# Two of 88 gathered edge groups fetched row by row from the sync and scalar engines in a graph network kernel

## What is computed

```python
h = jnp.maximum(_layernorm(x, axis=-1), 0.0)
x = x + _L0_gnn_ref(h, edge_index, ...)          # three SAGE layers: mean of neighbours, two products each
h = jnp.maximum(_layernorm(x, axis=-1), 0.0)
# the GINE block, the "edge stage" of the kernel:
messages   = gelu((h[src] + edge_attr) @ We1 + be1) @ We2 + be2
aggregated = segment_sum(messages, dst)
x = x + gelu(((1 + eps) * h + aggregated) @ Wu1 + bu1) @ Wu2 + bu2
```

## Time and profile before

| | |
|---|---|
| time, median of 3 runs (lowest to highest) | 881.31 us (880.73 to 883.44) |
| time of the profiled execution | 883.02 us |
| its span, first to last instruction | 880.7 us |
| granted TensorE clock, mean over the span | 0.983 |
| TensorE busy | 827.7 us (94%) |
| VectorE busy | 694.9 us (79%) |
| ScalarE busy | 323.9 us (37%) |
| GpSimd busy | 385.3 us (44%) |

### The profile page before, as it was taken

How to read it: one execution, slowest core, us unless ns; L and a number is a source line. 1 busy time by engine, 2 the same in 40 slices (tenths; PEclk the granted TensorE clock), 3 DMA queues, 4 the chain that set the end, 5 groups by cost and what they waited for, 6 DMA issues and landing times.

```text
span 880.7 us, 14779 instructions
## 1 busy us (share of the span) xinstructions
PE 827.7 (94%) x4876; PEld 631.4 (72%) x4876; DVE 694.9 (79%) x1887; ACT 323.9 (37%) x570; POOL 385.3 (44%) x443
## 2 busy tenths in 40 slices
PE   3688999999999999999889999999999999999994
PEld 1243555555687787777667888888888888898883
DVE  8999999998255445455799989988979898987961
ACT  3566677776155555454111111111121111112111
POOL 1000000000022222232578777777777777777772
PEclk9979999999999999999889999999999999999998
DMA  4301010001000000010563344444443444434421
GB/s 112 120 2 13 3 15 14 14 3 25 1 1 1 1 1 12 13 59 18 130 194 115 114 138 120 123 131 146 138 138 111 138 138 122 139 112 138 138 75 41
DMA packets 37492, 67.50 MB, mean 77 GB/s; under 512 B 14729, under 2 KB 24932, under 8 KB 37156
## 3 DMA queue, kind: packets, MB, share of 16 engines
q1 hardware_dynamic: 26276, 43.68, 16.6%
q0 software_dynamic: 11136, 22.83, 9.7%
HBM read 63.18 MB, written 3.30 MB: 75 GB/s over the span
## 4 chain that ended last, share of the span: by engine, by line
PE 41%; POOL 29%; DVE 13%; issue 11%; DMA 4%; ACT 1%; SPq 0%; POOLq 0%; ACTq 0%; DVEq 0%
POOL f_adj L653 29%; PE f_ps L1328 16%; PE f_ps L1321 10%; PE f_ps L1226 3%; PE f_ps L1219 2%; PE f_ps L1383 2%; DVE f_select L945 2%; PE f_ps L1295 2%; DVE f_region L722 2%; DMA inv<-f_rstd 2%; DVE f_region L720 2%; PE f_ps L1257 1%; DVE f_region L726 1%; DVE f_region L724 1%; PE f_ps L1425 1%
## 5 line engine op out<-in xcount | busy, mean ns | idle before, releaser
L653 POOL DMA_INDIRECT f_adj<-table,f_by_edge x348 | 333.4, 958 | 106.9 <-issue 103.9
L945 DVE TENSOR_SCALAR f_select<-f_ps 128x512 fp32r<-128x512 f32 x425 | 260.5, 678 | 6.6 <-PE f_ps L1383 6.0
L1383 PE MATMUL f_ps<-f_select,f_pair 125*128 125x512 f32 x850 | 220.8, 407 | 5.3 <-DVE f_select L945 5.2
L638 POOL CAST f_wide<-f_adj 125x500 fp32r<-125x500 uint8 (+1 forms) x70 | 40.6, 580 | 358.1 <-ACT f_adj L1091 212.4
L1383 PEld LDWEIGHTS f_ps<-f_select,f_pair 125*128 125x128 f32 x850 | 155.7, 190 | 44.7 <-issue 8.5
L1205 ACT ACTIVATE f_adj<-f_adj 128x512 f32<-128x512 f32 (+1 forms) x88 | 55.1, 626 | 306.4 <-DVE f_adj L1061 256.6
L1328 PE MATMUL f_ps<-f_wide,f_pair 125*128 125x500 f32 (+1 forms) x700 | 162.5, 385 | 1.5 <-DVE f_wide L777 0.6
L1091 ACT CAST f_adj<-f_ps 128x500 f32 x213 | 126.0, 592 | 55.8 <-PE f_ps L1226 43.4
L1328 PEld LDWEIGHTS f_ps<-f_wide,f_pair 125*128 125x128 f32 x700 | 122.2, 189 | 33.5 <-issue 6.2
L1425 PEld LDWEIGHTS f_ps<-f_adj 128*128 128x128 f32 x984 | 119.4, 192 | 13.1 <-issue 11.1
L1321 PE MATMUL f_ps<-f_adj,f_parts 125*128 125x500 fp8e4 (+1 forms) x525 | 128.5, 354 | 0.0
(11 more groups left out here) (149 smaller groups left out, 717.0 us busy)
## 6 DMA issues: line engine op xcount, KB each, us to landing
f_region<-in_edge_attr_T SPq DMA_DIRECT2D x33, 768.0 KB
f_adj<-table,f_by_edge POOLq DMA_INDIRECT x348
f_src_rows<-in_src_row SPq DMA_DIRECT2D x16, 256.0 KB, 4.7
f_xT<-in_xT SPq DMA_DIRECT2D x1, 1562.5 KB, 6.4
f_adj<-inv SPq DMA_DIRECT2D x1, 1562.5 KB, 9.4
out<-f_xT SPq DMA_DIRECT2D x6, 250.0 KB, 3.3
table<-f_region SPq DMA_DIRECT2D x6, 224.0 KB
f_rcntT<-inv SPq DMA_DIRECT2D x5, 250.0 KB, 3.7
```

What stands on the lines that cost most here:

```text
L653: pool.indirect_dma_start(out=rows[:, r % RW, j * D:(j + 1) * D], out_offset=None, in_=table, in_offset=bass.IndirectOffsetOnAxis(ap=table ...
L945: ins = dve.tensor_scalar(select[:, u % SELECT, :], offset, float(b * NP - CENTRE), None, ALU.is_equal)
L1383: ins = pe.matmul(z_columns(g), chosen[0:NP, p, b, :], select[0:NP, u % SELECT, :], start=b == 0 and p == 0, stop=b == NB - 1 and p == 1, ...
```

## The change

Groups 91 and 98 (`FAR`) no longer come by indirect DMAs, so GpSimd has 340 of them instead of 348. Each of their 1,024 rows comes by a DMA of its own, 1 partition x 128 floats, into a new buffer `far`.

```diff
+    FAR = [G - 14, G - 7]
+    FROM, UNTIL, BATCH = 2, G - 16, 8
+    ON_SP, FEW = 1, 4
...
+        far, o = carve(flat, o, (len(FAR), T * D), F32)
...
+            for i, g in enumerate(FAR):
+                sp.dma_start(far_idx[1:2, i * T * P:(i + 1) * T * P],
+                             t["src_row"][s.tile(g) * P:s.tile(g + 1) * P].rearrange("(a n) -> a n", a=1)
+                             ).then_inc(far_in, 16)
             sp.dma_start(inv.rearrange("(b p) -> p b", p=NP), rstd[0:NP, :],
...
+            def fetch_rows(k):
+                _, at_rows = nc.values_load_multi_w_load_instructions(
+                    far_idx[1:2, k * BATCH:(k + 1) * BATCH], engines=[mybir.EngineType.SP], min_val=0, max_val=N - 1,
...
+                for n, row in enumerate(at_rows, k * BATCH):
+                    i, j, p = n // (T * P), n // P % T, n % P
+                    sp.dma_start(far[p:p + 1, i, j * D:(j + 1) * D], table[bass.ds(row, 1), :]).then_inc(fetched[i], 16)
+
+            sp.wait_ge(far_in, 16 * len(FAR))
+            batches = ON_SP * T * P // BATCH
             for g in range(END):
+                if FROM <= g < UNTIL:
+                    for k in range((g - FROM) * batches // (UNTIL - FROM), (g - FROM + 1) * batches // (UNTIL - FROM)):
+                        fetch_rows(k)
...
-                if g in s.picked:
+                if g in s.picked or g in FAR:
                     continue
...
+                        if g in FAR:
+                            dve.wait_ge(fetched[FAR.index(g)], 16 * T * P)
+                            fetched_rows = far[:, FAR.index(g), 0:w]
...
+            few_from, few = ON_SP * T * P // FEW, (FAR_ROWS - ON_SP * T * P) // FEW
             for g in range(END):
+                if g == FROM:
+                    act.wait_ge(far_in, 16 * len(FAR))
+                if FROM <= g < UNTIL:
+                    for k in range((g - FROM) * few // (UNTIL - FROM), (g - FROM + 1) * few // (UNTIL - FROM)):
+                        fetch_rows(few_from + k)
                 for c in node_due(g, TAKE):
```

More of the change, by code:

```diff
@@ L251, in fast_path @@
     FLAG, KEEP = 12, 13
+    FAR = [G - 14, G - 7]
+    FROM, UNTIL, BATCH = 2, G - 16, 8
+    ON_SP, FEW = 1, 4
+    FAR_ROWS = sum(s.tiles(g) for g in FAR) * P
+    assert not any(g in s.picked or s.tiles(g) < T or g < UNTIL for g in FAR)
     with ExitStack() as ctx:
@@ L325, in fast_path @@
         viol, o = carve(flat, o, (4 * NT + 2 * G,), F32)
+        assert FAR_ROWS <= 4 * NT + 2 * G
+        far_idx = viol[:, 0:FAR_ROWS].bitcast(I32)
         bound, o = carve(flat, o, (2, G), F32)
@@ L378, in fast_path @@
             sem("node_added"), sem("stored"))
+        far_in, fetched = sem("far_in"), [sem(f"fetched{i}") for i in range(len(FAR))]
         tile_in, dst_tile_in, abs_ready = sem("tile_in"), sem("dst_tile_in"), sem("abs_ready")
@@ L587, in _ @@
             sp.dma_start(order[0:EP, 1, :], t["dst_next"]).then_inc(order_in, 16)
+            def fetch_rows(k):
+                _, at_rows = nc.values_load_multi_w_load_instructions(
+                    far_idx[1:2, k * BATCH:(k + 1) * BATCH], engines=[mybir.EngineType.SP], min_val=0, max_val=N - 1,
+                    skip_runtime_bounds_check_because="sources are node indices, as for the indirect DMAs")
+                for n, row in enumerate(at_rows, k * BATCH):
[3 more added lines that the diff above has]
+            batches = ON_SP * T * P // BATCH
             for g in range(END):
+                if FROM <= g < UNTIL:
+                    for k in range((g - FROM) * batches // (UNTIL - FROM), (g - FROM + 1) * batches // (UNTIL - FROM)):
+                        fetch_rows(k)
                 if g % PER == PER - 1 and EA < g // PER + EA < UNITS:
@@ L1057, in _ @@
                         dve.wait_ge(z_ready, g + 1)
-                        dve.wait_ge(gathered[r % RW], 16 * sum(s.tiles(s.of_ordinal(q)) for q in range(r % RW, r + 1, RW)))
+                        if g in FAR:
+                            dve.wait_ge(fetched[FAR.index(g)], 16 * T * P)
+                            fetched_rows = far[:, FAR.index(g), 0:w]
+                        else:
+                            gathers = [s.of_ordinal(q) for q in range(r % RW, r + 1, RW)]
+                            dve.wait_ge(gathered[r % RW], 16 * sum(s.tiles(h) for h in gathers if h not in FAR))
+                            fetched_rows = rows[:, r % RW, 0:w]
                         if r >= PR:
                             dve.wait_ge(msg_ready, s.of_ordinal(r - PR) + 1)
-                        dve.tensor_tensor(pre[:, r % PR, 0:w], z_group(g), rows[:, r % RW, 0:w],
+                        dve.tensor_tensor(pre[:, r % PR, 0:w], z_group(g), fetched_rows,
                                           ALU.add).then_inc(pre_ready, 1)
@@ L1181, in _, with fetch_rows @@
                     act.copy(part(chosen, 0, c), grow_rows(c)).then_inc(high3, 1)
-            for g in range(END):
+            def fetch_rows(k):
+                _, at_rows = nc.values_load_multi_w_load_instructions(
+                    far_idx[1:2, k * FEW:(k + 1) * FEW], engines=[mybir.EngineType.Activation], min_val=0, max_val=N - 1,
+                    skip_runtime_bounds_check_because="sources are node indices, as for the indirect DMAs")
+                for n, row in enumerate(at_rows, k * FEW):
+                    i, j, p = n // (T * P), n // P % T, n % P
+                    act.dma_start(far[p:p + 1, i, j * D:(j + 1) * D], table[bass.ds(row, 1), :]
+                                  ).then_inc(fetched[i], 16)
+            few_from, few = ON_SP * T * P // FEW, (FAR_ROWS - ON_SP * T * P) // FEW
+            for g in range(END):
+                if g == FROM:
[3 more added lines that the diff above has]
+                        fetch_rows(few_from + k)
                 for c in node_due(g, TAKE):
```

## The result

The changed kernel takes 915.72 us at the median (915.38 to 915.93, 4 runs) where the kernel before takes 882.13 (880.73 to 883.44, 4 runs) on the same chip: a ratio of 1.0377 [1.0363, 1.0392], 33.6 us slower. The forecast was 912 us, slower with 0.72.

The account below looks back on a forecast made before the run. TensorE was taken as the bound, only 3.0 us of its waits being winnable. The sum -3.0 + 33 + 0 = +30 on 883.0 us profiled gave 913 to 914, the median 1.7 lower: 912 us, range 878 to 948.

Parts of the forecast that it names:

- The bound of the gain, -3.0 us: At the end, eight gathers less save TensorE at most its 3.0 us of waits for the last messages.
- A batch on the scalar engine, 2.31 us: Scalar engine's sequencer: one register load (0.31 us) and four row issues (0.50 us each) take 2.31 us.
- The windows that are too short: From start of message h - 3 to picked group h's first product, batches don't fit at eleven of fifteen groups: 40 us.
- The place in the window: TensorE waits mostly at the first product behind the scalar engine's copy, which comes 2.8 us late at group 64.
- The size, +33 us: Late copies at eleven picked groups cost TensorE 40 us, less 7 us as the next windows open earlier.
- That the cost has a threshold: Scalar engine's batches: under 1.05 us each no window is too short; at 1.3 us copies are 3.0 us late.
- the issuing is hidden: Rival: batches fall into the scalar engine's 256.6 us of waits for the vector engine, leaving -3.0: 878 us; chance 0.14.
- SP at 0: SP's 64 batches, 276 us, are hidden in its 362.3 us wait for TensorE ahead of edge-attribute loads: 0 us.
- the queues at 0: DMA queues: 1,024 more packets, 91 us if one engine takes them all, are wanted only at groups 91 and 98: 0.
- The rule of the Trainium skill: By it the scalar engine's issuing would cost close to nothing, sum -3.0; the prediction went by the trace's rows instead.

Follow-up runs that it names:

- e3_no_fetch: Changed kernel with no row issued: two bulk loads of stand-in table rows fill `far` for groups 91 and 98; 879.82 us, 0.9977 of the kernel before.
- e1_sp_only: Changed kernel with group 98 given back to the gathers; only group 91's 512 rows are issued, by SP; 879.76 us, 0.9977 of the kernel before.
- e5_half_rows: Changed kernel with 64 scalar-engine batches instead of 128 over the same turns, stand-in rows for the rest; 880.59 us, 0.998 of the kernel before.
- e8_fixed_rows: Changed kernel with the scalar engine's 512 DMAs taking fixed table rows, without register load or address operation; 880.97 us, 0.998 of the kernel before.
- e9_split_640_384: e7_quiet_turns with 640 rows on SP and 384 on the scalar engine; 884.52 us, 1.0017 of the kernel before.
- e2_act_only: Changed kernel with group 91 given back to the gathers; only group 98's 512 rows are issued, by the scalar engine; 914.26 us, 1.0382 of the kernel before.
- e4_long_turns: Changed kernel with the scalar engine's 128 batches kept out of each picked group's turn and the turn ahead of it; 917.04 us, 1.0401 of the kernel before.
- e7_quiet_turns: Changed kernel with 768 rows on SP, 256 on the scalar engine, there only in turns where neither group nor next two are picked; 922.22 us, 1.0455.
- e6_sixteen_picked: e7_quiet_turns with 16 picked groups instead of 17; 923.23 us, 1.046 of the kernel before.
- e10_split_sixteen: e9_split_640_384 with 16 picked groups instead of 17; 884.37 us, 1.0015 of the kernel before.

## Why the prediction was right, and where it was not

- **The bound of the gain, -3.0 us: right.** Rows that cost nothing (`e3_no_fetch`) gain 2.1 us at the median, 3.1 in the span, though the last gather starts 10.7 us earlier. TensorE, not the engine that was relieved, is what the end depends on.
- **A batch on the scalar engine, 2.31 us: right, from parts that were not.** It takes 2.2 to 2.4. The address is 37 + 29 ns, not 147; an issue is 214 ns, not 290 (the first of a batch 446); but the register load grows with what it loads, 502 ns for four numbers where one took 278. The errors cancel, rounding too: the prediction's own terms add up to 0.52 us a row and 2.39 a batch, and it went on with 0.50 and 2.31. The Trainium skill (DMA: Bandwidth & Descriptors, Latency and other measured facts) has a floor of about 600 ns under a tensor_load; the loads of four rows here go down to 320 ns, those of eight are at 720.
- **The windows that are too short: right.** In both traces each window can be measured, from the start of message h - 3 to the first product. The eleven that the prediction found too short (9, 15, 27, 33, 45, 52, 58, 64, 76, 82, 88) grew by 5.6, 4.4, 5.2, 3.6, 2.1, 1.7, 1.9, 2.1, 5.3, 3.9 and 2.0 us, 38 in all where the sum said 40; of the other four only the one at 70 grew (0.9).
- **The place in the window, wrong.** "TensorE gets the copy 2.8 us late" and "most of it at the first product behind a copy" was the step that failed: 15.7 us are waited one step earlier, at the `flip`, for the gelu, and 4.9 at the product behind the copy. The batches of h - 2 and h - 1 already stand ahead of the gelu, and the prediction tested the window only at its end. That the waits at the `flip` are eleven as well is chance: they stand at nine of these groups and at 3 and 70, and none at 52 and 88.
- **The size, +33 us: the total right, its make-up not.** TensorE's idle time in the stage grows from 451 - 432.89 = 18.1 us to 484 - 444.80 = 39.2, so by 21 us, not by 33. The other 12 are matmuls that take longer. The 2,681 matmuls of the stage come in the same order in both traces, so they can be compared one by one: 7.3 us stand in those that overlap time at the lower clock (the sums above, 10.3 less 3.6, make this about 7 us), a term that the prediction didn't have, and 4.6 us in the 21 that follow a wait only after the change, 0.22 us each, since they no longer overlap with the one ahead of them. Without the clock's 7 us the loss would be some 27 us, an estimate from these figures; that the total comes within 4 us of the forecast is in part luck. That the lapses come from the waits is argued from where they stand, right behind late gelus and copies, and was not tried by itself. The runs agree with it: from 500 to 860 us the traces of `e1_sp_only`, `e3_no_fetch`, `e5_half_rows`, `e8_fixed_rows` and `e9_split_640_384` have none, those of `e2_act_only`, `e4_long_turns`, `e7_quiet_turns`, `e6_sixteen_picked` and `e10_split_sixteen` three, five, six, seven and one.
- **That the cost has a threshold: right.** The prediction's own rule said no loss under 1.05 us a batch and 3 us at 1.3; at 1.2 us (`e8_fixed_rows`) 2.0 us of waits at the gelu are left. The rival "the issuing is hidden" fails on the price and not on its logic: 211.5 us of the scalar engine's waits for sums are still there, in places where nobody is in a hurry.
- **SP at 0 and the queues at 0: right.** SP's wait for TensorE falls from 362.3 us to 139.7 in the profile after, and `e1_sp_only` loses nothing. With 96 batches instead of 64 (`e7_quiet_turns`) the cover is gone and TensorE waits 27.6 us for loads; the prediction had named this as the end of the cover, and put it at 9 us for 371 us of issuing. Each row is two packets, not the one that the prediction took, yet the 1,024 rows are 43 us of packet time (20 on q10, 23 more on q1), not 91.
- **The rule of the Trainium skill** (DMA: Bandwidth & Descriptors, Issuing engines are not separate DMA queues) that the time to start a DMA is usually small beside the DMA: for 512 DMAs of 0.5 KB with addresses from registers the trace does not agree: their start, register load and address included, brings the whole loss of 34 us. For the same DMAs with fixed addresses the result is the one by that rule, no loss.

## What to carry to other kernels

An engine whose arithmetic is idle for most of a stage has no room for work in its in-order list unless the idle time lies in front of things that nobody waits for; look for the tightest run of dependent instructions on it and ask whether one unit of the new work fits there, at each of its steps and not only at the last. Work of this kind costs nothing as long as it fits and what does not fit is paid, so halve it, or put it on the engine with one long slack (here SP, where 80 batches of 4.1 us cost next to nothing and 96 did not), before giving the idea up. And before building a way to relieve an engine, run the kernel with the relief for nothing: here that showed at once that at most 3 us were to be had.

## What the runs showed of the hardware beyond that

- A register load takes the longer the more numbers it loads: 278 ns for one, 502 for four on the scalar engine, 720 for eight on SP.
- The fused register operation ahead of a DMA takes 37 ns, and a move of 29 ns goes with it; the one of the adjacency stage takes 147.
- A one-row DMA from fixed addresses takes longer to issue (265 ns) than one whose address was put together ahead of it (214 ns, the first of a batch 446), and yet four of them are done in 1.17 us, not 1.55.
- TensorE's granted clock fell to 1.2 GHz four times for some 3 us, behind waits of 1.1 to 2.3 us; in the 3 us ahead of each fall the engine was busy for 1.3 to 1.6 us.
